# Second attention of a two-layer decoder block: query weights loaded a stage earlier, separate accumulator banks at its start and end, last statistics moved between the last outputs

## The reference

```
x = x + tanh(g_xattn[0]) * attention0(layernorm(x), ctx)      # 32 heads, 8 key heads, RMS norm inside
x = x + tanh(g_ffn[0])   * ffn0(layernorm(x))                 # linear + orthogonal Fourier update
x = x + tanh(g_xattn[1]) * attention1(layernorm(x), ctx)      # this case
x = x + tanh(g_ffn[1])   * ffn1(layernorm(x))                 # product in emulated fp8, one scale for all of x
```

```
q = Wq @ x + bq;  k = (Wk @ ctx + bk) @ proj_k;  v = (Wv @ ctx + bv) @ proj_v     # k, v: 64 columns
scores = einsum('bdhn,bdhk->bhnk', q, k) / HD ** 0.5       # 16 heads of 16 rows
prob = softmax(scores, axis=-1)
out = Wm @ einsum('bhnk,bdhk->bdhn', prob, v) + bm
```

## Time and profile of the kernel before

| | us |
|---|---|
| median of three runs | 1449.82 |
| the profiled execution | 1453.11 |
| its span in the profile | 1451.3 |
| PE busy in the span | 1345.4 (93%) |
| VectorE busy | 899.8 (62%) |
| ScalarE busy | 690.6 (48%) |
| middle stage's last product ends | about 1060 |
| attention 1 | 1065.5 to 1372.2 |
| last stage starts | 1372.5 |

### The profile page before, as it was taken

The page is one execution under the profiler, slowest core; times in us unless marked ns, Lnnn a source line. Parts: engine busy times, 40 slices in busy tenths (PEclk is TensorE's granted clock), DMA queues, the critical chain, the costliest instruction groups (busy, mean ns, idle before and its releaser), DMA issues. The chain is left out here.

```text
span 1451.3 us, 26112 instructions
## 1 busy us (share of the span) xinstructions
PE 1345.4 (93%) x9807; PEld 1048.3 (72%) x9815; DVE 899.8 (62%) x1451; ACT 690.6 (48%) x1762; POOL 280.8 (19%) x333
## 2 busy tenths in 40 slices
PE   6998799989999999987999999999968999998388
PEld 6998788879888898964788878888834455454144
DVE  4353377667767767665333245668846678885697
ACT  4221077766767777674111010103216666665296
POOL 0010001101010110011011014223222444443223
PEclk9999899999999999998999999999979999999789
DMA  6742564554535455473635446111335554443123
GB/s 227 254 154 77 108 143 111 140 133 102 139 82 145 113 141 156 102 204 111 227 124 194 162 142 253 37 58 45 94 87 124 119 119 104 100 103 85 48 98 145
DMA packets 137315, 185.44 MB, mean 128 GB/s; under 512 B 31703, under 2 KB 101463, under 8 KB 137200
## 3 DMA queue, kind: packets, MB, share of 16 engines
q1 hardware_dynamic: 137200, 183.82, 44.6%
HBM read 88.57 MB, written 35.29 MB: 85 GB/s over the span
## 5 line engine op out<-in xcount | busy, mean ns | idle before, releaser
L1151 ACT ACTIVATE a_prob<-a_psS,a_negmax 128x256 f32<-128x256 f32 x512 | 237.3, 484 | 153.9 <-DVE a_negmax L1063 153.9
L1063 DVE TENSOR_REDUCE a_negmax<-a_psS 128x4 f32<-128x1024 f32 x128 | 154.0, 1204 | 71.2 <-PE a_psS L956 69.6
L931 PE MATMUL a_psQ<-a_xT_hi,wide 128*128 128x256 f32 x912 | 171.0, 288 | 1.4 <-DVE a_q_lo L1058 1.0
L1378 PE MATMUL m_psY<-wide,m_a_hi 128*128 128x512 f32 x512 | 160.1, 394 | 6.8 <-DVE m_a_lo L1426 6.8
L1378 PE MATMUL m_psY<-w_ffn,m_a_hi 128*128 128x512 f32 x512 | 158.3, 390 | 0.0
L966 PE MATMUL a_psT<-ident,a_prob 128*128 128x128 f32 x1024 | 138.1, 279 | 14.8 <-issue 6.1
L931 PEld LDWEIGHTS a_psQ<-a_xT_hi,wide 128*128 128x128 f32 x912 | 138.8, 189 | 10.2 <-issue 5.8
L966 PEld LDWEIGHTS a_psT<-ident,a_prob 128*128 128x128 f32 x1024 | 116.8, 144 | 24.3 <-issue 13.1
L1168 ACT COPY a_probT<-a_psT 128x512 f32<-128x512 f32 x208 | 116.1, 611 | 37.1 <-PE a_psT L966 36.1
L931 PE MATMUL a_psQ<-a_xT_lo,wide 128*128 128x256 f32 x456 | 127.5, 280 | 0.0
L881 POOL COPY a_recip<-a_recip_head 128x256 f32<-128x256 f32 x64 | 25.7, 401 | 522.6 <-DVE a_recip_head L1114 522.6
(11 more groups left out here) (222 smaller groups left out, 2639.9 us busy)
## 6 DMA issues: line engine op xcount, KB each, us to landing
a_q_stack<-a_q_hi SPq DMA_DIRECT2D x128, 128.0 KB, 2.4
a_q_stack<-a_q_lo SPq DMA_DIRECT2D x128, 128.0 KB, 2.6
b_q_stack<-b_q_hi SPq DMA_DIRECT2D x128, 128.0 KB, 2.4
c_raw<-lay_ctxT SPq DMA_DIRECT2D x16, 512.0 KB, 4.9
rows<-in_x SPq DMA_DIRECT2D x8, 1024.0 KB, 6.7
scratch_o<-a_oT SPq DMA_DIRECT2D x16, 512.0 KB, 3.0
m_x<-in_x SPq DMA_DIRECT2D x8, 1024.0 KB, 5.9
scratch_x<-m_x SPq DMA_DIRECT2D x8, 1024.0 KB, 5.1
```

The lines of the kernel that those rows point to most:

```text
L931: last = nc.tensor.matmul(bank[:, 0:S], w[:, kt, t * P:(t + 1) * P], a[:, kt, :], start=(kt == 0 and w is wq.hi and a is xT_hi), stop=(kt ...
L1063: nc.vector.tensor_reduce(negmax[:, n % 2, :], psS[:, bank:bank + 2, :].rearrange("p a (j k) -> p (a j) k", k=S), AX_X, ALU.max, negate=Tr ...
L1151: last = nc.scalar.activation(prob[:, n % 2, j, :], psS[:, 2 * (n % 2) + j // 2, (j % 2) * S:(j % 2 + 1) * S], ACT.Exp, bias=negmax[:, n % ...
L1378: last = nc.tensor.matmul(psY[:, 2 * t + h, :], a[:, u, kt, rows_t], m[:, kt, cols], start=(kt == 0 and a is a_hi and m is w.hi), stop=(kt ...
```

## The change

It touches attention 1, and the part of the middle stage that loads small tables for it.

- The query weights are loaded in the middle stage by `Attn1Bias.load`, into a tile that is held to the end of attention 1; the wait for them at the start of attention 1 goes.
- The four queries of batch 0 are written to four banks: `psQ`, the two of `psP`, and `psO`. Their waits for the bank go. The start is written out: queries 0 and 1, two scores, query 2, two scores, two scores, query 3, two scores, then the transposes of the shift and four scores. The first turned scores wait for all four queries to be evicted. ScalarE evicts the shift ahead of query 3. VectorE's `low_keys(0)` moves behind `normalise_x2(1, 0)`.
- SyncE's list at the start is put in another order: keys, mask, row mask, the rows and values of batch 0, then the other tables. GpSimd waits for the mask alone.
- The steps of batch 8 go. In their place after the loop: outputs 0 and 1 of batch 7, the two spreads of reciprocals (the second into a bank of `psS`), outputs 2 and 3. Outputs 1 to 3 go to `psP` and `psO`. On VectorE the reciprocals come first, then the statistics of batch 6 with their aggregation, then `normalise_o`, then the rest of batch 6, and the first two statistics of batch 7 after three of its four additions. ScalarE takes the reciprocals' high part ahead of the outputs' evictions. GpSimd takes the root for batch 6 after the first addition.

```diff
-            sp.wait_ge(attn1_bias.loaded, 32)
+            sp.wait_ge(attn1_bias.loaded, 48)
...
         sp.dma_start(self.q[:, :], c["bq_col"]).then_inc(self.loaded, 16)
+        sp.dma_start(self.wq[:, :, :], c["wq1T"]).then_inc(self.loaded, 16)
...
-        STEPS = [(b, k) for b in range(-1, B + 1) for k in range(TILES)]
+        STEPS = [(b, k) for b in range(-1, B) for k in range(TILES)]
+        def query_bank(a, k):
+            return psQ[:, :] if a or k == 0 else psO[:, :] if k == 3 else psP[:, k - 1, :]
+        def output_bank(b, k):
+            return psQ[:, :] if b < B - 1 or k == 0 else psO[:, :] if k == 3 else psP[:, k - 1, :]
+        def spread_bank(b, h, t):
+            return psS[:, 0, :] if (b, h, t) == (B - 1, 1, 1) else psB[:, :]
...
-            sp.dma_start(wqT[:, :, :], c["wq1T"]).then_inc(wq_loaded, 16)
             load_keys(0)
-            for tile, name in ((mask, "head_mask"), (row_mask, "row_mask"), (sum_of, "sum_of"), (spread_raw, "spread")):
+            sp.dma_start(mask[:], c["head_mask"]).then_inc(mask_loaded, 16)
+            sp.dma_start(row_mask[:], c["row_mask"]).then_inc(consts_loaded, 16)
+            load_rows(0)
+            load_v1(0)
+            for tile, name in ((sum_of, "sum_of"), (spread_raw, "spread")):
                 sp.dma_start(tile[:], c[name]).then_inc(consts_loaded, 16)
...
+            low_reciprocals(B - 1, 1)
+            for k in range(TILES):
+                add_output(outputs + k, B - 1, *tile_of(k))
+                if k == 0:
+                    norm3.rstd_of(pool, B - 2, rms=False)
             norm3.rstd_of(pool, B - 1, rms=False)
...
+            first(0)
+            first(1)
+            for k in range(2):
+                for i in range(2):
+                    scores(0, k, i)
+                first(2 + k)
+                for i in range(2, 4):
+                    scores(0, k, i)
+            turn_shift(0, 0)
+            for i in range(4):
+                scores(0, 2, i)
...
+            for k in range(2):
+                for dt in range(CT1):
+                    output(outputs + k, B - 1, *tile_of(k), dt)
+            for t in range(CT1):
+                spread_reciprocals(B - 1, 1, t)
+            for k in range(2, TILES):
+                for dt in range(CT1):
+                    output(outputs + k, B - 1, *tile_of(k), dt)
...
-            stats_x3(B - 1)
+            reciprocals(B - 1, 1)
+            stats_x3(B - 2)
+            moments_x3(B - 2)
+            for t in range(CT1):
+                normalise_o(B - 1, 1, t)
+            keep_x3(B - 2)
+            for t in range(TT):
+                normalise_x3(B - 2, t)
+            for t in range(TT):
+                largest_x3(B - 2, t)
+            stats_x3(B - 1, TILES * B - 1)
+            dve.wait_ge(added, TILES * B)
             moments_x3(B - 1)
...
+            for k in range(3):
+                copy_query(0, k)
+            act.wait_ge(consts_loaded, 48)
+            act.wait_ge(ones_ready, 1)
+            high_keys(0)
+            copy_shift(0, 0)
+            copy_query(0, 3)
```

More of the change, by code:

```diff
@@ L1646, in sem @@
             return es.enter_context(nc.semaphore("b_" + name))
-        wqT = sb("wqT", [P, CT1, S])
         wmT = sb("wmT", [P, CT1, S])
-        bq, bm = bias.q, bias.out
+        bq, bm, wqT = bias.q, bias.out, bias.wq
         mask = sb("mask", [P, HT1, NK1])
@@ L1759, in _ @@
             for b, k in STEPS:
-                if k == 0 and real(b + 1):
+                if k == 0 and b >= 0 and real(b + 1):
                     load_rows(b + 1)
@@ L1827, in query @@
                 if dt == 0:
-                    if a == 0 and k == 0:
-                        pe.wait_ge(wq_loaded, 16)
                     pe.wait_ge(x2_norm.normed, 4 * a + 2 * h + 2)
+                if dt == 0 and a:
                     done = [output_of(*step)[0] for step in STEPS[:STEPS.index((a - 1, k)) + 1]]
@@ L1833, in query @@
                         pe.wait_ge(y_ready, sum(map(real, done)))
-                    elif TILES * a + k:
+                    else:
                         pe.wait_ge(q_ready, TILES * a + k)
-                last = nc.tensor.matmul(psQ[:, :], wqT[:, dt, t * P:(t + 1) * P], xn[:, dt, h * HALF_N:(h + 1) * HALF_N],
+                last = nc.tensor.matmul(query_bank(a, k), wqT[:, dt, t * P:(t + 1) * P], xn[:, dt, h * HALF_N:(h + 1) * HALF_N],
                                         start=(dt == 0), stop=(dt == CT1 - 1))
@@ L1910, in spread_reciprocals @@
                     pe.wait_ge(o_ready, 2 * n + 1)
+                bank = spread_bank(b, h, t)
                 for part in range(2):
-                    nc.tensor.matmul(psB[:, part * S:(part + 1) * S], spread[:, t, part, :], recip_hi[:, :], start=True, stop=False)
-                    last = nc.tensor.matmul(psB[:, part * S:(part + 1) * S], spread[:, t, part, :], recip_lo[:, :],
+                    nc.tensor.matmul(bank[:, part * S:(part + 1) * S], spread[:, t, part, :], recip_hi[:, :], start=True, stop=False)
+                    last = nc.tensor.matmul(bank[:, part * S:(part + 1) * S], spread[:, t, part, :], recip_lo[:, :],
                                             start=False, stop=True)
@@ L1928, in output, with first @@
                     last.then_inc(out_full, 1)
+            def first(k):
+                for dt in range(CT1):
+                    query(0, k, dt)
+            first(0)
[9 more added lines that the diff above has]
+                scores(0, 2, i)
             outputs = 0
-            for b, k in STEPS:
+            for b, k in STEPS[TILES:]:
                 sa, sk = scored_tile(b, k)
@@ L1937, in _ @@
                 if (b, k) == (0, 0):
-                    pe.wait_ge(consts_loaded, 64)
+                    pe.wait_ge(consts_loaded, 48)
                     pe.wait_ge(spread_ready, 1)
-                if asked and not turned:
-                    for dt in range(CT1):
-                        query(b + 1, k, dt)
                 for half in range(2):
@@ L1960, in _ @@
                 for dt in range(CT1):
-                    if asked and turned:
+                    if asked:
                         query(b + 1, k, dt)
@@ L2039, in largest_x3 @@
                                         apply_absolute_value=True)
-            normalise_x2(0, 0)
+            for h in range(2):
+                normalise_x2(0, h)
             for b, k in STEPS:
@@ L2045, in _ @@
                 scored, spreads = real(sa), real(sb_)
-                if b == -1 and k == 0:
-                    normalise_x2(0, 1)
                 if scored:
@@ L2069, in _ @@
                     moments_x3(b - 2)
-                if k == 1 and real(b + 1):
+                if k == (1 if b >= 0 else 2) and real(b + 1):
                     low_keys(b + 1)
@@ L2104, in copy_query @@
                 for dst in (q[:, k % 2, :], q_hi[:, k, :]):
-                    last = nc.scalar.activation(dst, psQ[:, :], ACT.Identity, bias=bq[:, t:t + 1])
+                    last = nc.scalar.activation(dst, query_bank(a, k), ACT.Identity, bias=bq[:, t:t + 1])
                 last.then_inc(q_ready, 1)
@@ L2140, in _ @@
             outputs = 0
-            for b, k in STEPS:
-                if (b, k) == (-1, 1):
-                    act.wait_ge(consts_loaded, 64)
-                    act.wait_ge(ones_ready, 1)
-                if (b, k) == (-1, 3):
-                    nc.scalar.copy(spread[:, :, :, :], spread_raw[:, :, :, :]).then_inc(spread_ready, 1)
+            for k in range(3):
[5 more added lines that the diff above has]
+            copy_query(0, 3)
+            nc.scalar.copy(spread[:, :, :, :], spread_raw[:, :, :, :]).then_inc(spread_ready, 1)
+            for b, k in STEPS[TILES:]:
                 ob, t, h = output_of(b, k)
@@ L2157, in _ @@
                 if real(ob):
-                    copy_output(outputs, t)
+                    copy_output(outputs, ob, t, h)
                     outputs += 1
@@ L2170, in _ @@
                     copy_o(b, k)
+            high_reciprocals(B - 1, 1)
+            for k in range(TILES):
+                copy_output(outputs + k, B - 1, *tile_of(k))
 def ffn1_stage(nc, sh, scratch, out, quant, x):
@@ L2405, in build @@
                 attn0_stage(nc, sh, a, scratch, wide, rows, norm)
+            attn1_bias.hold_queries(nc, es)
             with ExitStack() as held:
```

27 lines of the change are left out of this document (18 added, 9 removed).

## The result

The changed kernel takes **1440.39 us** (median of four runs, 1439.89 to 1441.05) against 1449.8 (1448.73 to 1450.27). The ratio is 0.9937, with a 95% interval of 0.9925 to 0.9949: 9.4 us less, between 7.4 and 10.9 by the interval. The forecast was 1439.6, in a range of 1437.0 to 1443.6. The profiled execution took 1441.05, its span is 1439.2.

The account below looks back on a forecast made before the run. TensorE bounds the loop, so only the ends can gain: start 4.6, clock -0.9, end 6.8, last stage -0.3, together 10.2 us. That gives 1442.9 profiled, 1439.6 us against the median, range 1437.0 to 1443.6.

Parts of the forecast that it names:

- What bounds the kernel: Attention 1's loop is bound by TensorE, so the change can act only at the start and the end.
- The weights: Start of attention 1: with query weights loaded a stage earlier, the first product starts 2.0 us earlier.
- Cost nothing: Middle stage: 13 us without SyncE issues cover the weights' transfer; without that cover it would cost 0.4 to 3.5 us.
- The banks: Start: four banks for the first queries make the second query complete 3.8 us earlier.
- What is late next: Start: SyncE's queue limits next; shift out 4.65 us earlier, first turned scores near 1088.0; start gains 4.6, bounds 2.1 and 4.7.
- The additional microsecond for landing without a gap: Start: the shift's DMAs following the stack's without the 0.85 us gap may add up to 1 us to 3.25.
- The clock in batch 0: First turned scores: a wider hole brings longer half clock, -0.9 us, bounds +1.7 and -5.7.
- the present dip: Kernel before, from 1094.00: 3.40 us at half clock in bounded work, booked as costing about 1.7 us.
- the later one: Changed kernel, first turned scores: 5.3 us at half clock, booked as losing 2.65 us.
- The 14.8 us that stood for the longest recovery: Half clock from 1069.00 to 1083.80 in the kernel before, taken as the upper end for the clock's recovery.
- The end: Last values to last stage: VectorE's new list laid end to end gains 6.8 us, bounds 5.3 and 7.4.
- The last stage: Starts at half clock either way; booked at -0.3 us, bounds +0.3 and -1.5.

Follow-up runs that it names:

- the second profile of before: The kernel before the change, unchanged, profiled again: 24.56 us from the barrier to the first turned scores.
- the hole filled: Changed kernel plus unread products in TensorE's idle time ahead of the first turned scores: 1437.36 us, ratio 0.9923 to the kernel before.
- the kernel with the end alone: Changed end, with weights, order and bank of the start as in the kernel before: 1442.33 us, ratio 0.9956 to the kernel before.
- the one with the start alone: Changed start, with the old steps of batch 8 as in the kernel before: 1446.92 us, ratio 0.9978 to the kernel before.
- the repeats: Two more profiles of the unchanged kernel before: 24.56 and 24.44 us from the barrier to the first turned scores.

## Why the prediction was right, and where it wasn't

- **What bounds the kernel.** Right. The loop's middle has the same profile, and all that changed is at its two ends. One more kind of place had to be counted: how long the loop's first steps run at half clock.
- **The weights.** First product 1.50 us behind the barrier, as forecast (about 1.45). "Cost nothing" in the middle stage is right: the DMA stood on the queue ahead of the load of W_base, SyncE then issued nothing for 12 us, the weights landed within 5.7 us, and the middle stage's first product to the barrier took 376.66 us against 376.60. With the weights' DMA back in attention 1 the median was 1440.16 us: of the 2.27 us by which the first product is earlier, 1.34 reached the turned scores, and no median shows them.
- **The banks.** The step that failed is the second query's being complete 3.8 us earlier, because the trace of before had it at half clock. Counted from the barrier, it is complete at 8.24 us in the changed kernel and at 12.53 in that trace, but at 10.80 in the second profile of before. The rows were read rightly; that they hold for every execution was assumed. In the other course, and by two of three profiles of before, the second query is at full clock already, and the whole start wins 2.4 instead of 4.6 us. The term had bounds of 2.1 and 4.7 from the clock in the kernel after; it wanted the same bounds from the clock in the kernel before. The change's worth is also in this: the second query no longer waits, and no profile of the new start had the late course. Seven profiles of it are few to show that it can't occur.
- **What is late next.** Right: SyncE's queue, first turned scores released by the shift's DMAs. The additional microsecond for landing without a gap didn't come (3.36 against 3.25).
- **The clock in batch 0.** -0.98 in the pair and -0.9 forecast, but by two errors that cancel: the present dip was booked at 1.7 and costs nearly nothing, and the later one at 2.65 and costs about 1.2 (255.0 against 253.8). The 14.8 us that stood for the longest recovery count from the first product; the clock was at half from 2.19 us ahead of the barrier, 20.5 us in all. The direction was right, and so was the fall ahead of the turned scores: the clock fell at 1082.0, 4.2 us ahead of the turned scores. With the hole filled it stayed up. What the Trainium skill says on idle gaps ("TensorE: Matmul & The Clock Gate", "Why this matters for your kernels") agrees: the fall stands among TensorE's waits of 1.15 and 2.01 us around the last scores of tile 2.
- **The end.** 6.81 against 6.8, step by step: statistics and aggregation done 4.50 us behind the reciprocal's start (4.63 forecast), outputs normalised at 5.67 (5.93), batch 6 normalised at 8.51 (8.2), its maxima at 10.8 (10.5), last normalisation begun at 14.96 (15.1). The single steps are off by up to 0.3 us, both ways. One detail came otherwise: the overlap with GpSimd fell on the small copy at 1347.03, which took 1.26 us instead of 0.16, and the normalisation behind it ran undisturbed at 1.52. The copy ends at 1348.29 and GpSimd's addition at 1348.26. That is the rule of "SBUF — State Buffer" in the Trainium skill, "Who interferes with whom", to the letter: whoever comes second is blocked until the first is through. The price was 1.1 us; 0.5 was booked.
- **The last stage.** -0.12 in the pair; over the table it is 78.3 to 79.1 in kernels with the same code there, in step with how late the clock comes back (13.7 to 15.3 us behind the stage's first VectorE instruction).
- **What was not forecast**: 1.38 us ahead of the barrier. The profiles of before reach it at 1065.50, 1065.56 and 1065.75, the other eleven at 1062.12 to 1065.87, on average 1063.9. The middle stage takes 376.4 to 377.1 us in all, so it lies in the context stage or attention 0, whose code is untouched. The early weights and the new start are not needed for it: the kernel with the end alone reaches the barrier at 1063.91, the one with the start alone at 1063.82. Whether any other part of the change is behind it, or the spread of executions alone, no run here separates. It is **open**, and it matters: the changed parts by the repeats give 7.3 and 7.7 us, the medians 9.4 (7.4 to 10.9).
- **The number.** 1439.6 against 1440.39 is nearer than the working deserves: a start booked 2 us too high, two errors on the clock that cancel, and something ahead of the barrier booked at nothing.

## What to carry to other kernels

Profile the kernel before twice or more before a wait is priced, and compare the granted clock at the place: a term that rests on half clock in one trace may be an execution's luck. Where an engine's list is the bound, lay the new list end to end from its rows; it came out to 0.1 us in 19, though single steps were off by 0.3. And once a start or an end is a chain of short waits, what TensorE does while it waits is part of the kernel: fillers that nobody reads, in places where it waits anyway, with the stacking DMAs reordered, gave 7.4 us more than the change's last state.

## What the runs showed of the hardware that I had not expected

- The same code reached full clock 7.4 or 18.3 us behind the same barrier, with the same first query; the late one was the execution in which the clock had fallen nearest to the barrier (2.19 us ahead, against 2.83 and 2.72). That is worth 2.6 us here, as the three profiles of before show.
- A copy of two columns took 1.26 us instead of 0.16 where it met GpSimd's addition. The smallest VectorE instruction can pay the whole price of the overlap.
- 3.4 us at half clock under fully listed TensorE work (PE busy 3.40 of 3.40 us) cost nothing that can be measured in the loop. A busy PE isn't by itself a bound.
